# New turns of GpSimd and VectorE with four x buffers, and the weight rows of a tile read back over DRAM by one transfer instead of two

## The reference

```python
A = lora_As[adapter_mapping]; Bm = lora_Bs[adapter_mapping]      # cond layer
y = x @ W.T + b + ((x @ A) @ Bm) * 2.0
res_hidden = y @ A_ffn.T            # (.., 64)
probs = softmax(y @ router_w.T)     # (.., 16)
topw, topi = top_k(probs, 2); topw = topw / (sum(topw) + 1e-6)
combine = sum(one_hot(topi) * topw)
delta = einsum('bse,bsr,eor->bso', combine, res_hidden, B)
x = x + y @ base_w.T + base_b + delta * 0.5
```

## Time and profile before

| | |
|---|---|
| median of 3 runs | 104.41 us (103.74 to 104.44) |
| the profiled execution | 103.44 us, of which the span is 101.6 us |
| TensorE (PE) busy | 97.4 us, 96% of the span, 576 matmuls |
| VectorE (DVE) busy | 65.1 us, 64% |
| ScalarE (ACT) busy | 39.8 us, 39% |
| GpSimd (POOL) busy | 18.7 us, 18% |
| DMA | 16.91 MB, mean 166 GB/s |

### The profile page before, as it was taken

The page is one execution under the profiler, slowest core; times in us unless marked ns, Lnnn a source line. Parts: engine busy times, 40 slices in busy tenths (PEclk is TensorE's granted clock), DMA queues, the critical chain, the costliest instruction groups (busy, mean ns, idle before and its releaser), DMA issues.

```text
span 101.6 us, 1806 instructions
## 1 busy us (share of the span) xinstructions
PE 97.4 (96%) x576; PEld 88.1 (87%) x576; DVE 65.1 (64%) x182; ACT 39.8 (39%) x97; POOL 18.7 (18%) x34
## 2 busy tenths in 40 slices
PE   5899999999999999999999999999999999999990
PEld 5799999999989999988988997899788788888990
DVE  2529999948567867959946735677368726656101
ACT  3404446885519726554435126120920604031000
POOL 5100003000397990070330061000000000000000
PEclk9999999999999999999999999999999999999999
DMA  2999789999854172592672280470065191940311
GB/s 42 321 318 377 225 182 372 340 424 422 230 96 68 26 216 58 168 267 68 182 254 59 79 231 1 117 205 6 14 165 165 20 266 46 239 170 0 110 52 52
DMA packets 8089, 16.91 MB, mean 166 GB/s; under 512 B 1475, under 2 KB 3907, under 8 KB 7952
## 3 DMA queue, kind: packets, MB, share of 16 engines
q1 hardware_dynamic: 7472, 16.40, 53.5%
q10 hardware_dynamic: 576, 0.39, 1.2%
q0 software_dynamic: 32, 0.00, 0.0%
HBM read 13.28 MB, written 2.16 MB: 152 GB/s over the span
## 4 chain that ended last, share of the span: by engine, by line
PE 71%; issue 11%; POOL 11%; DMA 3%; ACT 1%; DVE 0%; POOLq 0%
PE pair L771 69%; POOL x_lo L352 4%; POOL e_lo L370 4%; DMA w_raw_all<-w_cat 3%; POOL p_lo L364 2%; POOL p_hi L362 1%; PE pair L919 1%; PE pair L921 1%; ACT p_hi L418 1%; PE pair L939 1%; ACT w_hi_all L392 0%; DVE xn L765 0%; POOLq L361 0%
## 5 line engine op out<-in xcount | busy, mean ns | idle before, releaser
L771 PE MATMUL pair<-e_hi,w_hi_all 128*128 128x512 f32 (+1 forms) x72 | 27.2, 378 | 0.0
L771 PE MATMUL pair<-e_lo,w_hi_all 128*128 128x512 f32 (+1 forms) x72 | 26.7, 370 | 0.0
L771 PE MATMUL pair<-e_hi,w_lo_all 128*128 128x512 f32 (+1 forms) x72 | 26.6, 370 | 0.0
L771 PE MATMUL pair<-p_hi,x_hi 128*128 128x304 f32 x64 | 19.7, 308 | 0.2 <-POOL p_lo L364 0.2
L771 PE MATMUL pair<-p_lo,x_hi 128*128 128x304 f32 x64 | 19.4, 302 | 0.0
L771 PE MATMUL pair<-p_hi,x_lo 128*128 128x304 f32 x64 | 19.3, 302 | 0.0
L771 PEld LDWEIGHTS pair<-e_hi,w_lo_all 128*128 128x128 f32 x72 | 13.6, 188 | 2.6
L771 PEld LDWEIGHTS pair<-e_hi,w_hi_all 128*128 128x128 f32 x72 | 13.6, 188 | 2.4
L771 PEld LDWEIGHTS pair<-e_lo,w_hi_all 128*128 128x128 f32 x72 | 13.6, 189 | 1.8
L712 DVE TENSOR_TENSOR exp_raw_all<-w_raw_all 128x512 f32<-128x512 f32 x16 | 10.4, 689 | 7.5 <-DMA w_raw_all<-spill 7.5
L502 ACT ACTIVATE w_hi_all<-exp_raw_all 128x512 fp32r<-128x512 f32 x16 | 9.6, 627 | 13.8 <-DVE exp_raw_all L712 13.8
(11 more groups left out here) (107 smaller groups left out, 131.5 us busy)
## 6 DMA issues: line engine op xcount, KB each, us to landing
w_raw_all<-spill SPq DMA_DIRECT2D x16, 256.0 KB, 3.9
exp_raw_all<-experts SPq DMA_DIRECT2D x4, 512.0 KB, 8.7
xn<-x_n SPq DMA_DIRECT2D x4, 512.0 KB, 7.3
out<-xn SPq DMA_DIRECT2D x7, 256.0 KB, 4.0
w_raw_all<-w_cat SPq DMA_DIRECT2D x3, 552.0 KB, 6.8
xt_raw<-x_t SPq DMA_DIRECT2D x2, 512.0 KB, 6.3
xt_raw<-x_t SPq DMA_DIRECT2D x1, 1024.0 KB, 12.6
c_stack<-c_hi SPq DMA_DIRECT2D x7, 74.0 KB, 4.2
```

Of the source, the lines that this page charges most:

```text
L771: return nc.tensor.matmul(out_ap, lhs, rhs, start=first, stop=last)
```

## The change

- The read back from spill is one DMA for each tile (L311, twice, becomes one), with the source spill[t] of 2 rows, each repeated 64 times.
- x has four buffers instead of two; the third and fourth lie in blocks 2 and 3 of w_hi and w_lo, which are free after the fold. x_hi of tiles 2 and 3 comes right after the fold on ScalarE, x_lo on GpSimd.
- GpSimd makes the low parts of expert pieces 0, 1 and 3, VectorE that of piece 2; the waits of TensorE and VectorE follow.
- Tile 0's LoRA product is one pair of matmuls with 98 rows (c_hi at rows 0 and 32, c_lo at 64, bias rows at 96) instead of four pairs. c_stack of tile 1 gets its bias rows by the DMA as the others do, so that tile 1's product waits for it too.
- b2 is brought in by the first step of bias_part instead of a step of its own; b1 and b2 are loaded after the LoRA tables.
- c is made with all products of one kind together, so that lb_lo is needed last; VectorE's lb_lo comes after two of p_lo.
- The idle matmuls read a constant and are 13; the first high part on ScalarE is cut in two.

```diff
-WARM_UP = 11
+WARM_UP = 13
+XB = 4
@@ SP
-            sp.dma_start(b1_col[:, :], b1).then_inc(in_b, 16)
-            sp.dma_start(b2_row[:, :], b2).then_inc(in_b, 16)
             sp.dma_start(xt_raw[:, 0:2, :], x_t[:, 0:2, :]).then_inc(in_xt[0], 16)
...
+            sp.dma_start(b1_col[:, :], b1).then_inc(in_b, 16)
+            sp.wait_ge(first_set, 1)
+            sp.dma_start(b2_rows[0:1, SMALL:], b2).then_inc(in_b, 16)
...
-            sp.dma_start(c_stack[HR:HT, 2:NT, :].bitcast(F32),
-                         c_stack[HR:HT, 1:2, :].to_broadcast([2, NT - 2, W2N]).bitcast(F32)
+            sp.dma_start(c_stack[HR:HT, 1:NT, :].bitcast(F32),
+                         c_first[F_BIAS:FT, :].unsqueeze(1).to_broadcast([2, NT - 1, W2N]).bitcast(F32)
                          ).then_inc(stacked_bias, 16)
...
-                for a in range(2):
-                    sp.dma_start(weight_rows[a * RH:(a + 1) * RH, b, :, :],
-                                 spill[t, a].partition_broadcast(RH)).then_inc(spread[b], 16)
+                sp.dma_start(weight_rows[:, b, :, :], spill[t].unsqueeze(1).to_broadcast([2, RH, GC, P])
+                             ).then_inc(spread[b], 16)
@@ GpSimd
             lora_a_parts(1)
             x_lo_part(2)
+
+            pool.wait_ge(bpl_done, 1)
+            x_lo_part(3)
             lora_a_parts(2)
-            split_experts_lo(2)
-            x_lo_part(3)
+            split_experts_lo(0)
             lora_a_parts(3)
+            split_experts_lo(1)
             split_experts_lo(3)
             for t in range(4, NT):
+                lora_a_parts(t)
                 x_lo_part(t)
-                lora_a_parts(t)
@@ ScalarE
-                if t >= 2:
-                    act.wait_ge(pe_x, t - 1)
+                if t >= XB:
+                    act.wait_ge(pe_x, t - XB + 1)
...
-            act.wait_ge(pe_warm, 1)
+            act.wait_ge(in_xt[1], 16)
+            x_hi_part(2)
+            x_hi_part(3)
             split_experts(0)
-            split_experts(1)
-            act.wait_ge(bias_step, KC + 1)
-            nc.scalar.activation(bp_hi[:, :], bias_part[:, :], ACT.Copy).then_inc(bph_done, 1)
             act.wait_ge(pe_c, 1)
             nc.scalar.activation(c_hi[:, :], w2_cols(ps_c), ACT.Copy).then_inc(ch_done, 1)
-
+            act.wait_ge(bias_step, KC)
+            nc.scalar.activation(bp_hi[:, :], bias_part[:, :], ACT.Copy).then_inc(bph_done, 1)
@@ VectorE
-                    dve.wait_ge(spread[b], 32 * (t // NB + 1))
+                    dve.wait_ge(spread[b], 16 * (t // NB + 1))
...
-            split_experts_lo(0)
             lora_first_lo()
+            dve.wait_ge(first_set, 2)
+            dve.wait_ge(first_high, 1)
+            nc.vector.tensor_tensor(c_first[F_LOW:F_LOW + R, :], w2_cols(ps_c)[0:R, :],
+                                    c_first[0:R, :].bitcast(F32), ALU.subtract).then_inc(first_low, 1)
             stack_bias()
             lora_lo(1)
             read_z(0)
             route(0)
-            split_experts_lo(1)
+            split_experts_lo(2)
@@ TensorE, lora_first_product
                 pe.wait_ge(ht_done, 1)
-                pe.wait_ge(ch_done, 1)
-                part(ht_first_hi[:, :], c_hi, False)
-                pe.wait_ge(cl_done, 1)
-                part(ht_first_hi[:, :], c_lo, False)
-                pe.wait_ge(ht_first_done, 1)
-                part(ht_first_lo[:, :], c_hi, False)
+                pe.wait_ge(first_high, 2)
+                pe.wait_ge(first_low, 1)
                 pe.wait_ge(bias_rows, 1)
-                part(ones[HR:HT, :], c_stack[HR:HT, 1, :], True).then_inc(pe_z, 1)
+                nc.tensor.matmul(ps_z[0][:, z_small[0]:BANK], ht_first[:, :], c_first[:, 0:border],
+                                 start=False, stop=True, skip_group_check=True)
+                nc.tensor.matmul(ps_z[0][:, BANK:BANK + W2N - border], ht_first[:, :], c_first[:, border:],
+                                 start=False, stop=True, skip_group_check=True).then_inc(pe_z, 1)
@@ TensorE, lora_product
-                if t == 1:
-                    pe.wait_ge(bias_rows, 1)
-                else:
-                    pe.wait_ge(stacked_bias, 16)
+                pe.wait_ge(stacked_bias, 16)
```

More of the change, by code:

```diff
@@ L120, in adaln_ffn_kernel, with x_split @@
         rden = sb("rden", [P, 1])
+        def x_split(split, w_split):
+            return [split[:, b] for b in range(2)] + [
+                w_split[:, b, 0:D].rearrange("p (k n) -> p k n", k=KC) for b in range(2, XB)]
+        x_his, x_los = x_split(x_hi, w_hi), x_split(x_lo, w_lo)
         weight_rows = w_raw_all[:, 0:NB * GC * P].rearrange("p (a j n) -> p a j n", a=NB, j=GC)
@@ L842, in x_first @@
                 else:
[L843 removed]
+                    pe.wait_ge(x_done, 5 if t == 2 else 2 * t)
                 if t >= 2:
```

179 lines of the change are left out of this document (91 added, 88 removed).

## The result

| | kernel before | changed kernel |
|---|---|---|
| median of 5 runs | 104.41 us (103.41 to 104.64) | 159.86 us (159.17 to 160.71) |
| profiled run: time, span | 103.44 us, 101.6 us | 159.86 us, 157.9 us |
| mean granted clock of TensorE | 1.0 | 0.849 |

The ratio is 1.537, with a 95% interval of 1.527 to 1.547. The forecast was 152 us, with a range of 136 to 172.

What follows compares the result with a forecast made beforehand. TensorE bounds the kernel before; the order saves 1.4 us, but eight serial two-engine reads of 12.2 us from 33.2, other transfers and the last tile make a span of 149.6, forecast 152 us, range 136 to 172.

Steps and rivals of the forecast that it cites:

- missing landing in the view of DMA issues: At c_stack<-c_stack, whose source starts with 2 rows: taken as a sign that the new read uses 2 engines.
- 9.36: TensorE's period a tile in us, set against 12.2 us a read, and 7.2 with about 4 engines.

Runs made afterwards that it cites:

- run with three slow reads: Changed kernel with two reads a tile, but tiles 2, 4 and 6 read by the one transfer from 2 rows: 120.38 us, ratio 1.160.
- first and third run on the order: Changed kernel, two reads a tile: VectorE's experts piece after tile 1's routing, 0.9906; then also tile 0's rows earlier, GpSimd's tile 4 x before its last experts piece, 0.9866.
- second run on the order: Changed kernel, two reads a tile, VectorE's experts piece after tile 1's routing, and tile 0's routing transpose inside tile 2's first x product: ratio 0.9918.

## What to carry to other kernels

Before merging two transfers into one, look at the first dimension of the source as well as of the target: the merged transfer may have fewer rows to hand out than either half had, and the saved half microsecond of issuing is paid with most of the DMA engines (14 of 16 here). The mark by which a profile shows it is a DMA share near a small number of sixteenths in a window inside the transfer. A missing landing in the view of DMA issues is only a hint: in the run with three slow reads the ten reads of the old form have none either.

Cover is not a property of the kernel but of a place in it. Take TensorE's pace where the late thing is needed (5.6 us near the end here, not 9.36), and follow the whole loop back to what lets the next transfer be issued: the small store behind a large read adds next to nothing in bytes and still set the period.

## What the runs showed of the hardware that was not expected

- A small transfer behind a large one on few engines has to wait for it. 8 KB took 10.1 us in the median behind 512 KB on two engines, and moving it to ScalarE's queue was worth 18.3 us over eight tiles. There it landed in 4.1 to 4.7 us with a read in flight, against 2.2 us before.
- Each engine is slower when more of them carry the read: 26.5 GB/s each with 2, 21 with 4 (85 GB/s), at most 18 with 8, 17 with 16 (267 GB/s). From two engines to eight the DMA moves 2.75 times as much (53 and 146 GB/s, the latter with some other traffic in it), not four times. It is not the new form, since the two reads of before run at 264 GB/s with all 16, 16.5 for each. Nor is it crowding on one row: with more engines each row is read less often (64 times with 2 rows, 8 times with 16). Which part it is (the DRAM side or the partitions written) was not tried.
- VectorE and GpSimd hold each other up. VectorE's piece of experts takes 1.22 us where it runs without a piece of GpSimd's beside it (first and third run on the order), 2.2 where it begins during one. GpSimd's copy of 64 columns takes 0.24 us alone, and 1.23 beside VectorE's piece, in the rows above at 35.56. The Trainium skill (SBUF — State Buffer, "SBUF: two separate sides") tells of one pair of ports that the two share, held by one instruction to its end, also by a VectorE operation with two inputs in SBUF against a GpSimd operation that reads SBUF. The traces agree. In the second run on the order GpSimd's piece ends at 35.62, VectorE's, begun at 34.71, at 36.70, and GpSimd's copy at 36.79: each ends about its own time alone, or less, behind the one before. So what one loses depends on how much of the other's instruction is left when it begins; here 1.0 us and no more than GpSimd's 2.4.
